# Scores of an attention layer from high and low halves of q and k, and two moves in the step's order

## The reference

```python
def attn(x, w_kv_down, w_kv_up, w_q, w_out):          # 16 heads of 64
    kv = (x @ w_kv_down) @ w_kv_up
    k, v = kv[..., :1024], kv[..., 1024:]              # each (8, 512, 16, 64)
    q = x @ w_q
    att = einsum('bqhd,bkhd->bhqk', q, k) * 64 ** -0.5
    att = softmax(where(causal, att, -inf))
    return einsum('bhqk,bkhd->bqhd', att, v).reshape(8, 512, 1024) @ w_out

x = x + attn(layernorm(x), ...)
x = x + moe(layernorm(x), ...)   # 8 experts, hidden 512, top 2, silu(g) * u
```

## Time and profile before

| | |
|---|---|
| time, median of 3 runs | 983.69 us (982.68 to 984.45) |
| the profiled execution: its own time | 984.38 us |
| its span, first to last instruction | 982.4 us |
| mean granted TensorE clock, share of full speed | 0.967 |
| busy: PE, DVE, ACT, POOL | 92%, 64%, 60%, 51% |

### The profile page before, as it was taken

One profiled execution on the slowest core, in us unless ns is written; L12 is line 12 of the kernel. 1 busy time (PEld: TensorE's weight loads), 2 busy tenths in 40 slices (PEclk: granted clock), 3 DMA queues, 4 the chain that ended last, 5 costly groups with the idle time before them and its releaser, 6 DMA issues.

```text
span 982.4 us, 19420 instructions
## 1 busy us (share of the span) xinstructions
PE 901.4 (92%) x5614; PEld 620.0 (63%) x5615; DVE 626.5 (64%) x2379; ACT 585.4 (60%) x1483; POOL 502.7 (51%) x530
## 2 busy tenths in 40 slices
PE   3999999999999999999999999999717999999980
PEld 2566666666666666666666666656415888888870
DVE  2576677777767777776776777677563554554543
ACT  2676677677676677667677676677503454455440
POOL 2555554665566466556646655654642433434340
PEclk9999999999999999999999999999957999999995
DMA  7746500000000000000000000000001111111109
GB/s 214 305 179 242 188 1 1 10 9 6 1 15 9 1 10 12 4 4 15 6 2 12 9 4 6 12 6 2 22 17 42 47 43 41 43 46 42 46 22 256
DMA packets 43688, 47.99 MB, mean 49 GB/s; under 512 B 4431, under 2 KB 35156, under 8 KB 43488
## 3 DMA queue, kind: packets, MB, share of 16 engines
q1 hardware_dynamic: 35072, 21.58, 8.0%
q0 software_dynamic: 8544, 25.51, 6.9%
HBM read 19.48 MB, written 28.05 MB: 48 GB/s over the span
## 4 chain that ended last, share of the span: by engine, by line
PE 68%; issue 14%; POOL 9%; DVE 3%; DMA 2%; SPq 1%; ACT 1%; POOLq 1%; DVEq 0%
PE low_ps L923 15%; PE low_ps L912 9%; POOL expert_out L390 7%; PE mid_ps L850 7%; PE out_ps L930 6%; PE mid_ps L890 5%; PE top_ps L890 5%; PE mid_ps L852 5%; PE mid_ps L851 5%; PE top_ps L912 4%; PE low_ps L890 4%; PE mid_ps L912 1%; POOL gate_p L388 1%; SPq L267 1%; DVE prob L590 1%
## 5 line engine op out<-in xcount | busy, mean ns | idle before, releaser
L316 POOL TENSOR_TENSOR prob<-prob,row_inv 128x512 f32<-128x512 f32 (+3 forms) x256 | 321.3, 1256 | 291.5 <-DVE row_inv L597 290.8
L427 ACT ACTIVATE prob<-prob,neg_max 128x256 f32<-128x256 f32 (+3 forms) x512 | 281.0, 551 | 172.2 <-DVE neg_max L590 172.2
L923 PE MATMUL low_ps<-PT,v_sb 128*64 128x512 f32 (+3 forms) x1024 | 153.7, 443 | 2.4 <-ACT PT L433 2.4
L923 PEld LDWEIGHTS low_ps<-PT,v_sb 128*64 128x64 f32 x1024 | 68.4, 137 | 95.0 <-issue 65.0
L912 PEld LDWEIGHTS low_ps<-ident,prob 128*128 128x128 f32 x768 | 86.5, 140 | 60.2 <-issue 50.1
L912 PE MATMUL low_ps<-ident,prob 128*128 128x128 f32 x768 | 108.4, 277 | 3.1 <-DVE neg_max L590 2.4
L799 DVE TENSOR_TENSOR prob<-mid_ps,prob 128x512 f32<-128x512 f32 x71 | 49.1, 691 | 76.9 <-PE mid_ps L852 56.9
L427 ACT ACTIVATION_READ_ACCUMULATOR prob<-prob,neg_max 128x1 f32 x512 | 96.8, 189 | 0.0
L590 DVE CUSTOM_DVE_ANT_0 prob<-mid_ps,mask 128x128 f32<-128x128 f32 (+1 forms) x256 | 93.5, 420 | 1.2 <-PE mid_ps L890 0.8
L590 DVE CUSTOM_DVE_ANT_0 prob<-top_ps,mask 128x512 f32<-128x512 f32 x128 | 83.3, 688 | 12.3 <-PE low_ps L912 12.3
L390 POOL DMA_INDIRECT expert_out<-prob,meta_row x71 | 70.8, 997 | 37.6 <-issue 37.6
(11 more groups left out here) (160 smaller groups left out, 1740.3 us busy)
## 6 DMA issues: line engine op xcount, KB each, us to landing
routed_rows<-W_dn POOLq DMA_DIRECT2D x8, 2080.0 KB, 7.4
routed<-routed_rows SPq DMA_DIRECT2D x71, 65.0 KB, 1.8
W_ffn<-expert_out SPq DMA_DIRECT2D x8, 512.0 KB, 7.2
X<-in_L_attn_x SPq DMA_DIRECT2D x8, 256.0 KB, 5.6
W_ffn<-in_L_ffn_Wg SPq DMA_DIRECT2D x8, 256.0 KB, 5.2
W_ffn<-in_L_ffn_Wu SPq DMA_DIRECT2D x8, 256.0 KB, 5.4
W_dn<-in_L_ffn_Wd SPq DMA_DIRECT2D x8, 256.0 KB, 4.4
out<-X SPq DMA_DIRECT2D x4, 512.0 KB, 5.9
```

Of the source, the lines that this page charges most:

```text
L316: nc.gpsimd.tensor_tensor(p_pair(i), p_pair(i), row_inv[:, i, :].unsqueeze(2).to_broadcast([P, 2, P * (i + 1)]), ALU.mult).then_inc(S["nor ...
L427: nc.scalar.activation(p_at(i, h), p_at(i, h), ACT.Exp, bias=neg_max[:, i, h:h + 1], scale=-1.0, accum_out=row_sum[:, i, h:h + 1]).then_in ...
L923: last = nc.tensor.matmul(y_ps[h * HD:(h + 1) * HD, j * P:T], v_sb[:, half, j, o + h * HD:o + (h + 1) * HD], PT[:, h, j, j:NT, :].rearrang ...
```

## The change

The buffer of q and k gets a second half: high and low parts, both of type F32R. ScalarE's copy out of `mid_ps` now writes the high part (rounded by the copy). A new VectorE instruction, `qk_lo`, takes the high part from what still stands in `mid_ps` and writes the low part; it stands where the y copy stood on VectorE. The scores are three passes in place of one float32 product. The y copy goes to ScalarE, between the exponentials of tile 3 and the v copy. On TensorE the v chunk goes behind the transposes of tile 1, and everything that waited until `mid_ps` was copied (`qk_copied`) now waits for the low part (`qklo_done`). To make room, the layer-norm output `xn_sb` is laid into four unused blocks of PT, and `xn2T` into `outT`; `y_sb` takes its place in the expert loop.

```diff
-        qk_sb = sb("qk_sb", [P, 2, T])
+        qk_sb = sb("qk_sb", [P, 2, 2, T], F32R)
...
+        xn_sb = [PT[:, 0, j, i, :] for j, i in ((1, 0), (2, 0), (2, 1), (3, 0))]
+
+        xn2T = outT
...
-        hT_sb = [outT, xn2T]
+        hT_sb = [outT, y_sb]
...
-            def qk_copy(n):
+            def qk_hi(n):
 
                 seen(act, S["qk_ready"], n + 1)
-                nc.scalar.activation(qk_sb[:, :, :].rearrange("p a n -> p (a n)"), mid_ps[:, :], ACT.Copy).then_inc(S["qk_copied"], 1)
+                nc.scalar.activation(qk_sb[:, 0, :, :].rearrange("p a n -> p (a n)"), mid_ps[:, :], ACT.Copy).then_inc(S["qkhi_done"], 1)
+
+            def y_copy(n):
+
+                seen(act, S["y_ready"], n + 1)
+                nc.scalar.activation(y_sb[:, :], y_ps, ACT.Copy).then_inc(S["y_copied"], 1)
...
                 if nxt:
-                    qk_copy(n + 1)
+                    qk_hi(n + 1)
                 if cur:
                     exps(n, 3)
+                if prev:
+                    y_copy(n - 1)
                 if v:
                     v_copy(n + 3, (k + 3) % NP // NT, (k + 3) % NT)
...
-            def y_copy(n):
-
-                seen(dve, S["y_ready"], n + 1)
-                nc.vector.tensor_copy(y_sb[:, :], y_ps).then_inc(S["y_copied"], 1)
+            def qk_lo(n):
+
+                seen(dve, S["qkhi_done"], n + 1)
+                nc.vector.tensor_tensor(qk_sb[:, 1, :, :].rearrange("p a n -> p (a n)"), mid_ps[:, :],
+                                        qk_sb[:, 0, :, :].rearrange("p a n -> p (a n)").bitcast(F32), ALU.subtract).then_inc(S["qklo_done"], 1)
...
                 if cur:
                     inv(n, 2)
-                if prev:
-                    y_copy(n - 1)
+                if nxt:
+                    qk_lo(n + 1)
...
             def scores(n, i):
 
                 if i == 1:
-                    seen(pe, S["qk_copied"], n + 1)
+                    seen(pe, S["qklo_done"], n + 1)
...
-                for h in range(2):
-                    d = slice(h * HD, (h + 1) * HD)
-                    last = nc.tensor.matmul(scores_at(i, h), qk_sb[d, 0, i * P:(i + 1) * P], qk_sb[d, 1, 0:P * (i + 1)],
-                                            start=True, stop=True)
+                for k, (a, b) in enumerate(((0, 0), (0, 1), (1, 0))):
+                    for h in range(2):
+                        d = slice(h * HD, (h + 1) * HD)
+                        last = nc.tensor.matmul(scores_at(i, h), qk_sb[d, a, 0, i * P:(i + 1) * P], qk_sb[d, b, 1, 0:P * (i + 1)],
+                                                start=(k == 0), stop=(k == 2))
...
-                if v:
-                    seen(pe, S["qk_copied"], n + 2)
-                    v_chunk(n + 3, m + (k + 3) // NP, (k + 3) % NP // NT, (k + 3) % NT)
                 if cur:
                     transposes(n, 1)
+                if v:
+                    seen(pe, S["qklo_done"], n + 2)
+                    v_chunk(n + 3, m + (k + 3) // NP, (k + 3) % NP // NT, (k + 3) % NT)
```

More of the change, by code:

```diff
@@ L78, in layer @@
         PT = sb("PT", [P, 2, NT, NT, P])
-        qk_sb = sb("qk_sb", [P, 2, T])
+        qk_sb = sb("qk_sb", [P, 2, 2, T], F32R)
         v_sb = sb("v_sb", [P, 2, NT, T])
         y_sb = sb("y_sb", [P, T])
-        xn_sb = sb("xn_sb", [P, NT, C])
         xT_sb = sb("xT_sb", [P, 2, 2, P], F32R)
@@ L101, in layer @@
         routed = sb("routed", [P, K, NT, ROW])
-        xn2T = sb("xn2T", [P, T])
         before_bf = sb("before_bf", [P, P], BF16)
@@ L492, in _ @@
             exps(0, 2)
-            qk_copy(1)
+            qk_hi(1)
             for bank, t in step0:
@@ L565, in pre_norm @@
                 for t in range(NT):
-                    nc.vector.tensor_scalar(xn_sb[:, t, :], X[:, NT * b + t, :],
+                    nc.vector.tensor_scalar(xn_sb[t], X[:, NT * b + t, :],
                                             mv_a[:, t, 0:1], rstd_a[:, t:t + 1], ALU.subtract, ALU.mult).then_inc(S["xn_done"], 1)
@@ L602, in t_copy, with step @@
                 nc.vector.tensor_copy(pt_sb(i), pt_ps(i)).then_inc(S[f"t{i}_copied"], 1)
-            def y_copy(n):
-                seen(dve, S["y_ready"], n + 1)
-                nc.vector.tensor_copy(y_sb[:, :], y_ps).then_inc(S["y_copied"], 1)
-            def step(n, k, cur=True, prev=True, pre=None, post=None):
+            def qk_lo(n):
+                seen(dve, S["qkhi_done"], n + 1)
+                nc.vector.tensor_tensor(qk_sb[:, 1, :, :].rearrange("p a n -> p (a n)"), mid_ps[:, :],
+                                        qk_sb[:, 0, :, :].rearrange("p a n -> p (a n)").bitcast(F32), ALU.subtract).then_inc(S["qklo_done"], 1)
+            def step(n, k, cur=True, nxt=True, pre=None, post=None):
                 if cur:
@@ L730, in _ @@
             dve.wait_ge(S["base_set"], 1)
-            step(0, 0, prev=False)
+            qk_lo(0)
+            step(0, 0)
             for k in range(1, NP + 1):
@@ L738, in _ @@
             for k in range(1, NP):
-                step(NP * (B - 1) + k, k, post=B - 2)
+                step(NP * (B - 1) + k, k, nxt=k < NP - 1, post=B - 2)
                 if k in SPLIT_AT:
                     split_weights(k)
-            step(STEPS, NP, cur=False)
+            step(STEPS, NP, cur=False, nxt=False)
             post_x2(B - 1)
@@ L858, in pre_T @@
                 for t in range(NT):
-                    last = nc.tensor.transpose(post_ps[:, t * P:(t + 1) * P], xn_sb[:, t, :], ident[:, :])
+                    last = nc.tensor.transpose(post_ps[:, t * P:(t + 1) * P], xn_sb[t], ident[:, :])
                 last.then_inc(S["xT_ready"], 1)
@@ L904, in transposes @@
                 if i == 0:
-                    seen(pe, S["qk_copied"], min(n + 2, STEPS))
+                    seen(pe, S["qklo_done"], min(n + 2, STEPS))
                     seen(pe, S["v_copied"], NT if n == 0 else 0)
```

6 lines of the change are left out of this document (3 added, 3 removed).

## The result

| | before | changed |
|---|---|---|
| time, median (range) | 983.64 us (982.68 to 984.45) | 990.0 us (989.28 to 992.24, 4 runs) |
| ratio, 95% interval | | 1.0070 (1.0056 to 1.0084) |
| span of the profiled execution | 982.4 us | 988.5 us |
| mean granted TensorE clock | 0.967 | 0.965 |
| busy: PE, DVE, ACT, POOL | 92, 64, 60, 51% | 91, 66, 62, 51% |

A forecast was written before the change was run, and what follows sets the result against it. TensorE was taken to bound the step, other engines close behind. Full batches +2.8, first +0.3, last +0.5, prologue +2.1 and end +1.5 made +7.2: 991.6 us for the profiled execution, forecast 991, range 984 to 1002.

The forecast's parts named there:

- p: Plain attention step: change in its length, 0.28 - s for s up to 0.30; +0.04 us expected, never below -0.02.
- the hidden y copy: Plain step: the y copy on ScalarE adds 0.60 us but allows the projection at 445.30, before the v chunk's 445.36.
- The rivals on weight loads: Score passes: weight loads show in the passes, scores cost 0.60 us more than summed, whole some +45 (1028 us); chance 0.08.
- heads one after the other: Scores: the two heads don't run side by side in F32R, step +2.05 us, whole about +134 (1118 us); chance 0.07.
- The not-slower rival: V chunk behind its wait: 0.10 us less there and s of 0.37 or more, whole -1.7 (982 us); chance 0.15.
- s: Score tiles on TensorE: time saved per step by three F32R passes; 0.24 us taken, 0 to 0.40 kept possible.
- k = 2 and k = 6: Steps where the low part stands behind extra VectorE work: projection starts later, +0.31 us and +0.20 us.
- A full batch: Attention: five plain steps at 0.04, plus 0.31, 0.20 and -0.24, make +0.47 us; six of them +2.8.
- the uncovered y copy: Last batch: the y copy costs 0.3 us each in two steps that have no v chunk.
- k = 5: Step with routing work on TensorE between tile 3 and the projections: the full saving stays, -0.24 us.
- The prologue: Both TensorE waits for the q/k copy grow by 1.26 us, less 0.4 for shorter first scores: +2.1 us.
- The end: Attention's end: the y copy ahead of ScalarE's weight splits waits for the last values, output copy +1.5 us.

The follow-up runs named there:

- the kernels in halves: Changed kernel with the q/k copy (high part) and the low part each as two 512-column instructions, q first: 987.61 us, ratio 1.0051.
- in halves with the y copy on VectorE: Changed kernel with q/k copy and low part each as two 512-column instructions, and the y copy back on VectorE behind the low part: 983.09 us, ratio 1.0002.

## Why the forecast held, and where its terms didn't

**The step.** The saving (0.24 forecast, 0.25 measured), the bound by the copy, low part and v chunk (p = +0.04, measured +0.03) and the hidden y copy were right, and the runs with two passes, with float32 scores and with the v chunk ahead each came out at the times that this reading gave. The rivals on weight loads and on heads one after the other are out with the 2.11 us of the scores. The not-slower rival needed s of 0.37 or more and 0.10 less at the v chunk; with two passes s was 0.46, and a plain step changed by -0.02 and not by -0.12.

One path in it was wrong, without harm to the number. I had TensorE, not kept waiting, at the v chunk 7.40 us into the step (444.33 - 436.93), so that 0.2 to 0.3 us of wait would show there. In the kernels in halves, where the low part is early, it is there only at 7.55, since the row maxima hold the projection at 3.27 us whatever the scores take: of the 0.25 only 0.07 are left behind that wait. At the v chunk 0.13 us of wait remain (7.68). So a low part that is never waited for brings 0.17 a step (10.14 for 10.31, in halves with the y copy on VectorE), and no more.

**k = 2 and k = 6 were over-charged**, by 0.12 each. I let the low part start at the recorded end of the reciprocal, and let VectorE gain 0.22: it starts 0.08 us earlier than that end, and VectorE gained 0.26. A full batch costs +0.16 on average (0.03, 0.04 and the others of the table), not +0.47, and six of them 1.0, not 2.8. The first batch came at 0.4 for 0.3. The last batch cost 0.1 in place of 0.5: the uncovered y copy is there (+0.26 in one step), but k = 5 gained 0.36. The steps together made 1.4 us of the 3.6 that I had for them.

**The prologue came out at +3.2 for +2.1 in this pair of traces.** The two longer waits are there (+1.3 each). The first projection ran at full speed in place of half (-0.9). The scores of step 0 take 1.0 less, where I had 0.4: 0.55 of it is the first tile, now at full speed (0.43 for 0.98 us), and 0.5 are the next two, mostly at half speed in both kernels. The v chunks ran mostly at half in place of full (+1.3), and the second projection's beginning too (+0.3). Another 0.9 is the first projection's start, 20.79 for 19.89; it lies between 19.37 and 21.17 in the traces of all these kernels, and the kernel before has 19.89 and 20.09, so I count it as no effect of the change. The sum had no term for the clock. How much of it is the change's is not shown: from the first projection to the scores of step 1 the kernel before takes 16.16 us here and 15.74 in another trace, the changed kernel 18.44, and the kernel with the y copy on VectorE, whose v chunks ran at full clock on the same prologue, 17.68. That is +1.5 or +1.9, beside the 2.1 of the sum.

**The end** was right to 0.1 in its mechanism (+1.5 for the output copy behind y copy and splits). The clock stands beside it twice: the last values at full speed (-1.7), the expert loop's beginning at half for 9 us longer (+1.7). Neither is shown to be the change's. The kernel before has the first at 2.38 us in another trace, and two kernels with the low part (y copy on VectorE, whole and in halves) have the half clock at the tail for 30.7 us, as the kernel before has it.

Steps +1.4, prologue +3.2, end +1.5 - 1.7, expert loop +1.7 are +6.1, the growth of the span; 7.2 was forecast. The mechanism held, but part of the agreement in the total is luck, errors of opposite sign: 2.2 too much in the steps against 1.1 too little in the prologue, and -1.7 against +1.7 for the clock at the end. What stays open is the clock's part on average: the kernels' own runs spread by 2 to 4 us, and the stretches of half clock lie differently in each trace.

## What to carry to other kernels

Where several engines are within 0.3 us of the bound, as here, making the bounding engine faster may only buy a wait; sum the chain of every engine through the step first, at each place where the bounding engine waits for another, and give the saved time a place where it can show. Work put on a chain between two engines can be split, so that the second half of the first instruction covers the first half of the next (0.13 us earlier at the v chunk here); where nothing waits on the halves, the split costs a little (0.06). A product that waits for its operand pays its weight load behind the wait too. Before moving small VectorE work into an idle stretch, compare its length with the stretch, and look at what GpSimd does in it. And before a stretch of half clock is put down to a change, look at a second trace of the same program.

## What the hardware showed that I had not expected

- VectorE's instruction of 8 elements lasted 1.38 us in place of 0.17 beside GpSimd's scaling of 1.89 us, with no idle time shown.
- A product that waits for the operand it streams (`y_sb`) costs 0.10 us more (1.12 for 1.02) than one whose operand is there: the load of its weights, ready long before, stands behind the wait too.
- VectorE's low part started 0.05 and 0.07 us behind the start of a reciprocal whose row lasts 0.13 and 0.16.
- The last values product took 4.07 us mostly at a granted clock of 1.2 GHz, and 2.38 at 2.4, in two traces of the same program.
- The idle 1.49 us of TensorE in the middle of the attention was followed by 3.4 us at half clock in four of six batches, and not in the other two.
